# Quantised attention: where the probability-value products stand beside the transposes of turned tiles

## The chip, the cores and the metric

The kernel runs on one core of one Trainium2 chip. The metric is the device time of one execution in microseconds (us), lower is better. A core has a matmul engine (TensorE, PE in the profile, whose weight loads are shown as PEld), VectorE (DVE), ScalarE (ACT), GpSimd (POOL), and SyncE (SP), which here issues the DMAs. Each engine works through its own list of instructions in program order and waits on semaphores where it needs the work of another.

## The reference

Two layers over x (16 x 256 x 512) with a context (16 x 256 x 512). The first layer is where the change lies: two attentions of 16 heads with 32 channels each, both with fake-quantised q, k, probabilities and v.

```
def _attn(x, ctx, wq, wk, wv, wo, bo, dq, dk, dv, dw):
    q, k, v = heads(x @ wq), heads(ctx @ wk), heads(ctx @ wv)
    sim = einsum('bhid,bhjd->bhij', _fq(q, dq, 128, 8), _fq(k, dk, 128, 8)) * SCALE
    attn = softmax(sim)
    out = einsum('bhij,bhjd->bhid', _fq(attn, dw, 0, 8), _fq(v, dv, 128, 8))
    return merge_heads(out) @ wo + bo
h1 = _ln(x, ln1);  x = _attn(h1, h1, a1) + x
h2 = _ln(x, ln2);  x = _attn(h2, context, a2) + x
h3 = _ln(x, ln3);  x = gated feed-forward(h3) + x
```

The second layer is a plain cross attention of 8 heads with 64 channels each.

## The kernel before

**Stages.** The program has three stages, one behind the other, each over all 16 sequences: both quantised attentions (0 to about 1224 us), the first half of the feed-forward (to about 1826 us), and its second half together with the second layer (to the end). The change is in the first stage only.

**Phases and groups.** In the first stage a phase is the inner part of one attention of one sequence: eight groups (GROUPS) of two heads. For every group TensorE makes the scores (`pe_scores`, L503) in one of two PSUM tiles S; DVE takes the row maxima (L690), POOL makes the bias, ACT the exponentials with their sums (`act_exp`, L595), POOL and DVE the scaled and rounded probabilities pq (`dve_probs`, L698 to L715), SP turns them by a DMA transpose into pT (`turn_probs`, L916), and TensorE makes the products of probabilities and values (`pe_pv`, L525) in a PSUM tile O, three groups behind the scores.

**Fills.** The wide work of TensorE, projections (L157), output projections (L148) and transposes of 128 x 128 blocks (L132), is cut into "fills" of half a tile and laid into the groups by tables. Fill j = 0 goes to the PSUM bank PJ0 and j = 1 to PJ1 (for q2 the other way round). One round of the loop treats two phases, first `two_` (second attention of one sequence), then `one_` (first attention of a later sequence):

```
PHASE2_FILLS = {0: [("q1", 0)], 1: [("q1", 1)], 2: [("k1", 0)], 3: [("k1", 1)],
                4: [("ctxT", 0), ("ctxT", 1), ("o1", 0)], 5: [("o1", 1)], 6: [("v1", 0)], 7: [("v1", 1)]}
PHASE1_FILLS = {0: [("h2T", 0), ("h2T", 1), ("k2", 0)], 1: [("q2", 0)], 2: [("q2", 1)], 3: [("k2", 1)],
                4: [("o2", 0)], 5: [("o2", 1)], 6: [("v2", 0)], 7: [("hT", 0), ("hT", 1), ("v2", 1)]}
```

The fills ctxT, h2T and hT are the turned tiles: eight transposes of the context, of the normalised second input (from xhat of x1) and of the normalised next sequence (from xhat of x_in). `act_transposed` takes their first half out of PJ0 (L579 as a copy for ctxT; through `affine_act`, L179, for the others), and `dve_transposed` their second half out of PJ1 (L671, or `affine_dve`, L186). Both come in their engine's list ahead of the exponentials and the probabilities of the same group. xhat of x1 (`ln_xhat`, L124) comes in DVE's list at the end of group 7 of `two_`.

**Rounds.** Around the loop of 13 rounds stand the phases P_A and P_B ahead of it, a peeled round, and P_Y and P_Z behind it, with tables of their own. P_A has ctxT in group 4, P_B has h2T in group 5 and hT in group 7, P_Y has ctxT in group 0 and h2T in group 5.

**Order of TensorE in a group** (`pe_phase`): the scores of the next group; then the fills that are transposes; then the products of the group three back; then the other fills. A fill waits until its PSUM bank is emptied (`pj_emptied`), a transpose for its source as well, the products for the turned probabilities (`probs_turned`). A matmul that waits holds up all that stands behind it in this list.

Of the kernel before, what the change touches and what calls it, by code (L numbers as in the profile page):

```python
# [39 lines left out]
def build(nc, t, out):  # L40
# [3 lines left out]
    def sb(stack, name, shape, dt=F32):  # L44
        return stack.enter_context(nc.sbuf_tensor(name, shape, dt))
# [7 lines left out]
    with ctx:  # L53
# [73 lines left out]
        def transpose_chunks(bank, src, j):  # L127

            for c in range(2):
                for tt in range(TT):  # L130
                    k = 2 * j + c
                    last = nc.tensor.transpose(bank[:, c * TOK + tt * P:c * TOK + (tt + 1) * P],  # L132
                                               src[:, tt, k * P:(k + 1) * P], ident[:])
            return last
# [10 lines left out]
        def by_token(bank, w, xT, j):  # L145

            for k in range(KC):
                last = nc.tensor.matmul(bank[:], xT[:, k, j * P:(j + 1) * P], w[:, k, :],  # L148
                                        start=(k == 0), stop=(k == KC - 1))
            return last  # L150
# [79 lines left out]
        def bank_of(stage, name, j):  # L230

            return 1 - j if name == "q2" else j
# [4 lines left out]
        def before(stage, b, name, j):  # L237

            bank = bank_of(stage, name, j)
            n = fills_of(stage, bank).index((name, j))  # L240
            if stage != "first":
                n += len(fills_of("first", bank))
                n += len(fills_of("loop", bank)) * (b if stage == "loop" else ROUNDS)
            if stage == "last":
                n += len(fills_of("peeled", bank))
            return n
# [3 lines left out]
        def kind_of(name):  # L250
            return name.split("@")[0]
# [28 lines left out]
        def at(stage, b, name, j):  # L280
            return (stage, b, name, j)
# [13 lines left out]
        def turned_before(stage, b, name, j, kinds=TURNED):  # L295

            def those(s, fills=None):
                return [f[0] for f in (ORDER[s] if fills is None else fills)
                        if f[1] == 0 and kind_of(f[0]) in TURNED]
            n = 0  # L300
            if stage != "first":
                n += len(those("first")) + len(those("loop")) * (b if stage == "loop" else ROUNDS)
            if stage == "last":
                n += len(those("peeled"))
            here = those(stage, ORDER[stage][:ORDER[stage].index((name, j))])
            while here and kind_of(here[-1]) not in kinds:
                here.pop()
            return n + len(here)
# [26 lines left out]
        with ExitStack() as one:  # L335
# [12 lines left out]
            hT = sb(one, "hT", [P, 2, KC, TOK], F32R)  # L348
            ctxT = sb(one, "ctxT", [P, 2, KC, TOK], F32R)
# [90 lines left out]
            def ln_x1(b):  # L440
                return 2 * b + 2 if not (isinstance(b, int) and b == B - 1) else 2 * b + 1

            def ln_x(b):
                return 2 * b - 1


            def wait_weight(pe, name):

                pe.wait_ge(w_low_done, KC * (WEIGHTS.index(name) + 1))

            def pe_fill(pe, where):
                stage, b, name, j = where
                kind = kind_of(name)
                bank = bank_of(stage, name, j)
                n = before(*where)
                if not (isinstance(n, int) and n == 0):

                    pe.wait_ge(pj_emptied[bank], n)
                if kind == "hT" or kind == "h2T":
                    seq = {"hT@0": 0, "hT@1": 1, "hT": b + 3, "h2T": b + 1}[name]  # L460
                    m = 0 if name == "hT@0" else (1 if name == "hT@1" else (ln_x(seq) if kind == "hT" else ln_x1(seq)))
                    pe.wait_ge(ln["xhat_done"], TT * (m + 1))
                    ins = transpose_chunks(PJ[bank], xhat, j)
                elif kind == "ctxT":
                    seq = 0 if stage == "first" else b + 1
                    pe.wait_ge(ctx_loaded, 16 * (seq + 1))
                    ins = transpose_chunks(PJ[bank], ctx_in, j)
                elif kind in ("o1", "o2"):

                    if stage == "first":  # L470
                        done = 1
                    elif name == "o2@15":
                        done = 32
                    elif stage == "last":
                        done = 30 if kind == "o1" else 31
                    else:
                        done = 2 * b + (2 if kind == "o1" else 3)
                    pe.wait_ge(oT_done, 2 * done)
                    if stage == "first":
                        pe.wait_ge(wo_loaded[0], 16)  # L480
                    ins = by_token(PJ[bank], wo[0 if kind == "o1" else 1], oT, j)
                else:

                    from_ctx = kind in ("k2", "v2")
                    pe.wait_ge(turned_low_done, 2 * turned_before(*where, ("ctxT",) if from_ctx else ("hT", "h2T")))
                    w = "a" + kind[1] + "_w" + kind[0]
                    if stage == "first":
                        wait_weight(pe, w)
                    ins = (by_token_split if kind[0] == "v" else by_channel_split)(
                        PJ[bank], w1[w], ctxT if from_ctx else hT, j)  # L490
                ins.then_inc(pj_filled[bank], 1)

            def pe_scores(pe, ph, g):

                pe.wait_ge(quantised, ph.q_at[g // (GROUPS // 2)])
                if not (isinstance(ph.n, int) and ph.n == 0 and g < 2):

                    pe.wait_ge(exp_done, 4 * (ph.group(g) - 1))
                for i in range(2):
                    h = 2 * g + i  # L500
                    r = DH0 * (h % 4)
                    for qt in range(TT):
                        ins = nc.tensor.matmul(S[g % 2][:, i, qt, :],  # L503
                                               qT[ph.tiles][r:r + DH0, h // 4, qt * P:(qt + 1) * P],
                                               kT[ph.tiles][r:r + DH0, h // 4, :], start=True, stop=True)
                ins.then_inc(scores_done, 1)
# [6 lines left out]
            def pe_pv(pe, ph, g):  # L513
                pe.wait_ge(probs_turned[g % 2], turned_count(ph, g))
                if g == 0:
                    pe.wait_ge(quantised, ph.v_at)
                half = g // (GROUPS // 2)
                if g % (GROUPS // 2) == 0 and not (isinstance(ph.n, int) and ph.n == 0):

                    pe.wait_ge(oT_done, 2 * ph.n + half - 1)  # L520
                for i in range(2):
                    h = 2 * g + i
                    r = DH0 * (h % 4)
                    for kc in range(TT):
                        ins = nc.tensor.matmul(O[half][r:r + DH0, (h // 4) % 2, :],  # L525
                                               vQ[ph.tiles][:, kc, h * DH0:(h + 1) * DH0],
                                               pT[:, g % 2, 4 * i + kc:4 * i + kc + 3:2, :], start=(kc == 0),
                                               stop=(kc == TT - 1))
                ins.then_inc(pv_done, 1)

            def pe_phase(pe, ph, prev, nxt):
                for g in range(GROUPS):
                    if g + 1 < GROUPS:
                        pe_scores(pe, ph, g + 1)
                    elif nxt:
                        pe_scores(pe, nxt, 0)
                    fills = ph.steps(g)
                    for name, j in fills:
                        if kind_of(name) in ("hT", "h2T", "ctxT"):
                            pe_fill(pe, at(ph.stage, ph.b, name, j))  # L540
                    if g >= 3:
                        pe_pv(pe, ph, g - 3)
                    elif prev:
                        pe_pv(pe, prev, g + GROUPS - 3)
                    for name, j in fills:
                        if kind_of(name) not in ("hT", "h2T", "ctxT"):
                            pe_fill(pe, at(ph.stage, ph.b, name, j))

            def pe_drain(pe, ph):

# [1240 lines left out]
```

## Time and profile before

| | us |
|---|---|
| median of 3 runs | 3019.38 (3018.3 to 3019.39) |
| the profiled execution: its own time | 3019.96 |
| the profiled execution: span from first to last instruction | 3018.2 |
| PE busy over the span | 2806.9 (93%) |
| DVE busy | 1771.2 (59%) |
| ACT busy | 1455.2 (48%) |
| POOL busy | 692.1 (23%) |

The shares are means over three stages with different limits. In the first stage alone (0 to 1224 us) PE is busy for 1079.50 us and DVE for 1045.49 us. A busy PE is one with a matmul under way, not one at its peak.

### The profile page before, as it was taken

How to read it: one execution, taken by the hardware profiler on the slowest of the kernel's cores; microseconds unless marked ns; L12 is line 12 of the kernel's file. 1: busy time of each engine (PE TensorE's matmuls, PEld its weight loads, DVE VectorE, ACT ScalarE, POOL GpSimd, SP SyncE). 2: the span in 40 equal slices, each digit the busy share in tenths (PEclk: the TensorE clock that was granted, in tenths of full speed). 3: DMA queues.
4: the chain of work that ended last, by engine and by line, in shares of the span. 5: the costliest groups of instructions: out<-in, count | busy, mean ns of one | idle time of the engine just before them, and what ended most of it. 6: DMA issues, size and time to landing. Idle time of an engine off the chain costs nothing. (4 is left out here: it accounts for less than half of the span.)

```text
span 3018.2 us, 54146 instructions
## 1 busy us (share of the span) xinstructions
PE 2806.9 (93%) x17920; PEld 2214.6 (73%) x17920; DVE 1771.2 (59%) x4484; ACT 1455.2 (48%) x3763; POOL 692.1 (23%) x1147
## 2 busy tenths in 40 slices
PE   5799999999999996699999997999999999999997
PEld 5566666666666663599999996888888888888885
DVE  6799899999999986433333335344444444444432
ACT  4577777777777765211111112444444444444442
POOL 1222222222222221133333322112111111111110
PEclk8899999999999997799999998999999999999997
DMA  4443343333333342400010004000000000000000
GB/s 144 83 82 80 80 85 85 79 84 85 83 80 80 87 77 54 152 29 28 28 42 28 28 21 140 22 28 35 28 28 28 28 28 28 28 28 28 35 15 14
DMA packets 325753, 169.11 MB, mean 56 GB/s; under 512 B 274240, under 2 KB 290624, under 8 KB 325696
## 3 DMA queue, kind: packets, MB, share of 16 engines
q1 hardware_dynamic: 325696, 168.39, 22.0%
q8 instruction: 31, 0.51, 0.1%
q14 instruction: 26, 0.21, 0.0%
HBM read 76.07 MB, written 25.17 MB: 34 GB/s over the span
## 5 line engine op out<-in xcount | busy, mean ns | idle before, releaser
L595 ACT ACTIVATE e<-S,bias,qk_scale 128x256 f32<-128x256 f32 x1024 | 563.6, 564 | 65.3 <-DVE e L707 61.4
L690 DVE TENSOR_REDUCE negmax<-S 128x4 f32<-128x1024 f32 x256 | 312.0, 1219 | 105.3 <-PE S L503 103.7
L707 DVE TENSOR_SCALAR e<-e,rsum 128x256 f16<-128x256 f32 x1024 | 291.8, 348 | 2.5
L565 ACT ACTIVATE shifted<-PJ,round_col,inv 128x512 f32<-128x512 f32 x192 | 149.4, 778 | 227.5 <-PE PJ L157 226.5
L1584 POOL TENSOR_TENSOR mid_partsB<-mid_actB,mid_partsB 128x256 fp32r<-128x256 f32 x128 | 102.1, 797 | 611.8 <-DVE mid_partsB L1482 611.8
L148 PE MATMUL PJ<-w_a_wo,oT 128*128 128x512 f32 x512 | 239.6, 612 | 2.6 <-ACT oT L604 1.8
L157 PE MATMUL PJ<-hT,w_a_wq 128*128 128x256 f32 x1536 | 208.3, 294 | 21.5 <-DVE hT L685 17.7
L157 PEld LDWEIGHTS PJ<-hT,w_a_wq 128*128 128x128 f32 x1536 | 195.4, 199 | 35.5 <-issue 35.5
L595 ACT ACTIVATION_READ_ACCUMULATOR e<-S,bias,qk_scale 128x1 f32 x1024 | 209.1, 204 | 0.0
L157 PE MATMUL AG0A<-h_partsA,upA 128*128 128x256 f32 x1536 | 200.0, 287 | 7.2 <-POOL h_partsA L1579 3.4
L157 PE MATMUL AG0B<-h_partsB,upB 128*128 128x256 f32 x1536 | 199.1, 286 | 7.6 <-POOL h_partsB L1579 6.4
L157 PEld LDWEIGHTS AG0A<-h_partsA,upA 128*128 128x128 f32 x1536 | 192.1, 194 | 15.7 <-issue 10.0
L157 PEld LDWEIGHTS AG0B<-h_partsB,upB 128*128 128x128 f32 x1536 | 192.4, 192 | 11.6 <-issue 8.1
L157 PE MATMUL AG1A<-h_partsA,upA 128*128 128x256 f32 x1536 | 195.9, 284 | 4.4 <-DVE downA L1429 4.4
L157 PEld LDWEIGHTS AG1A<-h_partsA,upA 128*128 128x128 f32 x1536 | 193.2, 193 | 8.7 <-issue 4.8
L157 PEld LDWEIGHTS AG1B<-h_partsB,upB 128*128 128x128 f32 x1536 | 191.6, 191 | 9.2 <-issue 5.0
L157 PE MATMUL AG1B<-h_partsB,upB 128*128 128x256 f32 x1536 | 195.8, 284 | 0.0
L1584 POOL TENSOR_TENSOR mid_partsA<-mid_actA,mid_partsA 128x256 fp32r<-128x256 f32 x128 | 100.5, 785 | 383.8 <-DVE mid_partsA L1482 383.8
L793 POOL TENSOR_TENSOR bias<-negmax,qk_scale 128x4 f32<-128x4 f32 x256 | 76.3, 298 | 460.5 <-DVE negmax L690 457.1
L148 PEld LDWEIGHTS PJ<-w_a_wo,oT 128*128 128x128 f32 x512 | 93.8, 192 | 112.0 <-issue 108.0
L1374 ACT ACTIVATE gateA<-AG0A,cols_pack 128x256 f32<-128x256 f32 x64 | 30.4, 475 | 270.6 <-PE AG0A L157 270.6
L1475 DVE SCALAR_TENSOR_TENSOR mid_actB<-AG1B,cols_pack,gateB 128x256 f32<-128x256 f32 x64 | 31.0, 484 | 210.7 <-ACT gateB L1374 210.7
(186 smaller groups left out, 5578.8 us busy)
## 6 DMA issues: line engine op xcount, KB each, us to landing
x_in<-in_x_dram SPq DMA_DIRECT2D x16, 512.0 KB, 3.5
ctx_in<-in_ctx_dram SPq DMA_DIRECT2D x16, 512.0 KB, 3.5
mid_dram<-x SPq DMA_DIRECT2D x16, 512.0 KB, 2.7
y_inA<-mid_dram SPq DMA_DIRECT2D x16, 512.0 KB, 3.6
part_dram<-x3A SPq DMA_DIRECT2D x16, 512.0 KB, 4.0
y_inB<-mid_dram SPq DMA_DIRECT2D x16, 512.0 KB, 3.2
kv_in<-in_ctx_dram SPq DMA_DIRECT2D x16, 512.0 KB, 4.7
baseB<-part_dram SPq DMA_DIRECT2D x16, 512.0 KB, 3.2
```

Of the source, the lines that this page charges most:

```text
L148: last = nc.tensor.matmul(bank[:], xT[:, k, j * P:(j + 1) * P], w[:, k, :], start=(k == 0), stop=(k == KC - 1))
L157: last = nc.tensor.matmul(acc, lhs(l), rhs(r), start=(start and i == 0), stop=(stop and i == 2))
L565: nc.scalar.activation(shifted[:, bank, :], PJ[bank][:], ACT.Identity, bias=round_col[:, 0:1], scale=inv[:, d:d + 1]).then_inc(pj_emptied[ ...
L595: nc.scalar.activation(e[:, s, i, :], S[s][:, i // 2, i % 2, :], ACT.Exp, bias=bias[:, s, i:i + 1], scale=qk_scale[:, ph.a:ph.a + 1], accu ...
L690: nc.vector.tensor_reduce(negmax[:, g % 2, :], S[g % 2][:].rearrange("p i q n -> p (i q) n"), AX_X, ALU.max, negate=True).then_inc(max_don ...
L707: nc.vector.tensor_scalar(e16[:, s, i, :], e[:, s, i, :], rsum[:, s, i:i + 1], ROUND16, ALU.mult, ALU.add).then_inc(prob_scaled, 1)
L793: nc.gpsimd.tensor_tensor(bias[:, g % 2, :], negmax[:, g % 2, :], qk_scale4[:, ph.a, :], ALU.mult).then_inc(bias_done, 1)
L1374: nc.scalar.activation(gate[:, f % 2, :], AG[f % 2][:, TOK:2 * TOK], ACT.Gelu, bias=ff_b1[:, c:c + 1]).then_inc(gate_done, 1)
L1475: nc.vector.scalar_tensor_tensor(out=mid_act[:, f % 2, :], in0=AG[f % 2][:, 0:TOK], scalar=ff_b1[:, c:c + 1], in1=gate[:, f % 2, :], op0=A ...
L1584: nc.gpsimd.tensor_tensor(mid_parts[:, f % 2, 1, :], mid_act[:, f % 2, :], mid_parts[:, f % 2, 0, :], ALU.subtract).then_inc(mid_low_done, 1)
```

## The change

In every group of `pe_phase` the products of probabilities and values come directly behind the scores, and all fills of the group, transposes first as the tables list them, come behind the products. No instruction is added or taken away, and no other engine's list is changed. Groups without transposes keep their order.

```diff
                     elif nxt:
                         pe_scores(pe, nxt, 0)
-                    fills = ph.steps(g)
-                    for name, j in fills:
-                        if kind_of(name) in ("hT", "h2T", "ctxT"):
-                            pe_fill(pe, at(ph.stage, ph.b, name, j))
                     if g >= 3:
                         pe_pv(pe, ph, g - 3)
                     elif prev:
                         pe_pv(pe, prev, g + GROUPS - 3)
-                    for name, j in fills:
-                        if kind_of(name) not in ("hT", "h2T", "ctxT"):
-                            pe_fill(pe, at(ph.stage, ph.b, name, j))
+                    for name, j in ph.steps(g):
+                        pe_fill(pe, at(ph.stage, ph.b, name, j))
```

## Rows read from the trace of the kernel before

**Rows 1.** The page: TensorE's granted clock in 40 slices, tenths of full speed.
```profile
PEclk8899999999999997799999998999999999999997
```

**Rows 2.** Windows, two rounds: length; busy PE, PEld, DVE, ACT, POOL; clock, DMA, GB/s.
```profile
507.00:576.30 69.30, 65.16 (x426) 44.17 (x424) 64.01 (x165) 51.60 (x153) 17.78 (x41) 1.00 0.39 83
576.30:647.00 70.70, 66.62 (x427) 45.69 (x425) 64.04 (x165) 51.67 (x153) 18.23 (x41) 0.98 0.38 82
```

**Rows 3.** Waits, 141 to 1093 us: who waited for whom, us in total, times, longest.
```profile
PE PJ L132 <- DVE xhat L124: 27.8, 14, 2.0
PE PJ L157 <- DVE turned L186: 9.9, 13, 0.8
PE PJ L132 <- ACT shifted L565: 9.3, 13, 0.7
PE PJ L157 <- ACT turned L179: 6.6, 13, 0.5
PEld PJ L148 <- ACT turned L579: 3.0, 14, 0.2
ACT turned L579 <- PE PJ L132: 2.9, 14, 0.2
```

**Rows 4.** Timeline of PE, ctxT: start, us, what, count, [idle before <- releaser].
```profile
506.71 0.39 PE L503 MATMUL S<-kT,qT 32*128 32x256 bf16 x4
507.03 1.29 PE L132 MATMUL PJ<-ident,ctx_in 128*128 128x128 f32 x8
508.25 0.40 PE L525 MATMUL O<-pT,vQ 128*32 128x256 bf16 x4
508.57 3.70 PE L148 MATMUL PJ<-w_a_wo,oT 128*128 128x512 f32 x8
```

**Rows 5.** Timeline of ACT beside it.
```profile
506.83 0.78 ACT L565 ACTIVATE shifted<-PJ,round_col,inv 128x512 f32<-128x512 f32 x1 [0.18 <-PE PJ L157]
507.82 0.59 ACT L579 COPY turned<-PJ 128x512 f32<-128x512 f32 x1 [0.21 <-PE PJ L132]
```

**Rows 6.** Timeline of DVE between ctxT and h2T, the last wait and xhat.
```profile
516.94 1.22 DVE L690 TENSOR_REDUCE negmax<-S 128x4 f32<-128x1024 f32 x1 [0.64 <-PE S L503]
...
525.20 0.99 DVE L124 TENSOR_SCALAR xhat<-x,mv,rstd 128x512 f32<-128x512 f32 x2
```

**Rows 7.** Timeline of PE at h2T.
```profile
526.25 1.10 PE L132 MATMUL PJ<-ident,xhat 128*128 128x128 f32 x8 [1.98 <-DVE xhat L124]
...
528.18 3.12 PE L157 MATMUL PJ<-ctxT,w_a_wk 128*128 128x256 f32 x24 [0.51 <-ACT turned L179]
```

**Rows 8.** Timeline of ACT at h2T.
```profile
527.03 1.02 ACT L179 ACTIVATE turned<-PJ,cols_pack 128x256 f32<-128x256 f32 x2 [2.38 <-PE PJ L132]
```

**Rows 9.** Timeline of PE at hT.
```profile
555.88 1.09 PE L132 MATMUL PJ<-ident,xhat 128*128 128x128 f32 x8 [0.72 <-ACT shifted L565]
...
558.06 3.01 PE L157 MATMUL PJ<-w_a_wv,ctxT 128*128 128x512 f32 x12 [0.76 <-DVE turned L186]
```

**Rows 10.** SP's issue of turned probabilities; their landing, 590 to 736 us.
```profile
520.06 1.23 SPq L916 DMA_TRANSPOSE pT<-pq  x1
...
DMA to landing us min/median/max: 3.0/3.1/3.7
```

**Rows 11.** Windows with a fallen clock, columns as in rows 2.
```profile
176.00:178.00 2.00, 1.49 (x13) 1.05 (x13) 1.94 (x3) 1.25 (x3) 1.44 (x2) 0.89 0.70 131
...
1016.00:1018.00 2.00, 1.49 (x11) 1.04 (x10) 1.83 (x4) 1.86 (x4) 0.88 (x2) 0.81 0.57 105
```

**Rows 12.** Timeline of PE at h2T in two rounds with a fallen clock.
```profile
597.49 4.60 PE L157 MATMUL PJ<-ctxT,w_a_wk 128*128 128x256 f32 x24 [0.51 <-ACT turned L179]
...
1085.95 1.94 PE L132 MATMUL PJ<-ident,xhat 128*128 128x128 f32 x8 [2.02 <-DVE xhat L124]
...
1088.37 4.87 PE L157 MATMUL PJ<-ctxT,w_a_wk 128*128 128x256 f32 x24
```

**Rows 13.** Timeline of PE in P_Y, behind ctxT and its products.
```profile
1125.85 0.40 PE L503 MATMUL S<-kT,qT 32*128 32x256 bf16 x4 [2.85 <-ACT e L595]
```

## The prediction

> **What bounds the kernel now.** I read the page's clock line first. Its dips lie at the ends of stages, with short ones inside the first stage [rows 1]. Then I cut the first stage into rounds. A round of the loop lasts 69.30 us and TensorE is busy for 65.16 of them, DVE for 64.01; the next one lasts 70.70 with the same number of instructions to within one or two and a lower mean clock [rows 2]. So TensorE is the bound with DVE close behind, and what matters is TensorE's idle time. The table of waits over all rounds shows four kinds of it, each once a round: 27.8 us in front of the transposes of h2T (for DVE's xhat), 6.6 us behind them (for ACT to empty PJ0), 9.3 us in front of those of hT (for ACT), 9.9 us behind them (for DVE) [rows 3]. The timelines of single places then tell what each gate hangs on.
>
> **What the change moves.** In a round the four matmuls of one product group trade places with eight transposes at three points: h2T, hT, ctxT. A product group takes the issue of 0.32 us (508.25 to 508.57), as the scores do (506.71 to 507.03) [rows 4]. Nothing is added, so each point is a question of which gate ends last.
>
> h2T, 14 times (13 rounds and the peeled one). The products move into the idle time of 1.98 us in front of the transposes [rows 7]. They can run there: their turned probabilities were issued at 520.06 and land within 3.0 to 3.7 us [rows 10], so at 523.8 at the latest, while the products will stand at 526.25 - 1.98 = 524.3. Were they late, 1.65 us of the idle time would cover it. The transposes start with xhat, as before. Behind them k2 starts at 528.18, for it waits until ACT has emptied PJ0: ACT starts 0.78 us after the transposes' start and needs 1.02 us, to 528.05, and 0.13 later k2 starts [rows 7, 8]. That chain does not contain the products. Before, they lay inside it and cost nothing; now they lie in front of it and cost nothing. Idle time behind the transposes grows from 0.51 to 0.83 us, that in front shrinks from 1.98 to 1.65. Gain: 0. Bounds: a gain of 0.32 us if something in the chain behind should be quicker, no loss.
>
> hT, 14 times (P_B too). The same figure: 0.72 us idle in front, for ACT to empty PJ0, and 0.76 behind, for DVE to empty PJ1; v2 starts at 558.06, 2.18 us after the transposes' start [rows 9]. The products fit into the 0.72. Gain: 0, bounds again 0 to 0.32.
>
> ctxT. Here there is no idle time in front: scores, transposes, products and o1 stand behind one another at 506.71, 507.03, 508.25 and 508.57 [rows 4]. The gate of o1 is again PJ0, emptied by ACT's copy. ACT stood idle for 0.21 us until TensorE had filled it, started at 507.82, and took 0.59, to 508.41 [rows 5]; with the 0.13 to 0.16 us that such a gate takes, o1 was released at about 508.55, just when the products had been issued. The table says so for all rounds: o1's weight load waits 0.2 us for this copy 14 times, and the copy itself 0.2 us for the transposes 14 times [rows 3]. The products are now exactly the cover of that copy. Moved ahead of the transposes, they push the transposes from 507.03 to 507.36; the copy ends at 508.74, o1 starts at about 508.90. Cost: 0.33 us. Bounds: 0 (if the gate hides something the timeline does not show), 0.40 (the full duration of a product group, [rows 4]). I take 0.33, since both sides of the gate were tight.
>
> Is this slip given back later in the round? It would be if TensorE's wait for xhat, 1.98 us, took it up. DVE's last wait before xhat is the row at 516.94, for TensorE's scores of group 7; from there DVE works without a wait to xhat at 525.20 [rows 6]. Those scores stand behind o1, so they, xhat and the transposes of h2T all come 0.33 us later. From k2 on TensorE runs again into its own list. The slip stays, once in each of 14 rounds: 14 x 0.33 = 4.6 us.
>
> The edges. In P_A and at h2T in P_B TensorE waits long in front of the transposes, and the products move into that: 0. In P_Y, ctxT has no cover: the next scores wait for ACT's exponentials [rows 13], which stand behind the copy, so 0.2 to 0.3 us: I take 0.2. Queues: SP issues a transfer only when products two groups back are done; these now end earlier at h2T and hT and at ctxT too, so nothing of SP's or POOL's comes later for them. DVE's half of ctxT was at its start held by DVE's own maxima, and has a wait for scores behind it; it takes the delay up.
>
> **The clock.** The granted clock falls to the lower level, 1.2 GHz of 2.4, behind h2T: windows of seven rounds, every other one, from 176 to 1016 us have a mean between 0.89 and 0.81 [rows 11], and the peeled round at 1086 us has slow matmuls too [rows 12]. What TensorE did before is the same each time: two idle stretches, 1.98 and 0.51 us, with 1.4 us of transposes and products between. Rounds in between have the same stretches and keep 2.4 GHz, so this is a margin. A fall costs 70.70 - 69.30 = 1.40 us [rows 2]; k2 then takes 4.60 us [rows 12] where it takes 3.12 [rows 7]. In the peeled round the transposes took 1.94 us instead of 1.09 and k2 4.87 [rows 9, 12], together 2.6 us more. So 8 falls in 14 rounds cost 7 x 1.40 + 2.6 = 12.4 us. The regular "every other" hangs on the length of two rounds (140.0 us); a round 0.33 us longer breaks it. The sum of idle time at h2T stays 2.48 us but TensorE now works for 1.1 us rather than 1.4 between the two stretches, so they lie closer. I take two falls more: 2 x 1.40 = 2.8 us. Bounds: 0 falls (-12.4 us) and 14 (+8.4 us).
>
> The Trainium skill speaks against the change here. "TensorE: Matmul & The Clock Gate", section "A second HAM failure mode: psum-queue depth-cycling", says that micro-idles between groups of matmuls can be frequent enough for the clock to swing between its levels. The change adds a micro-idle of 0.33 us at ctxT and doesn't shorten the sum at h2T. By that rule every h2T would be followed by a fall, which is rival C; the trace so far agrees only in that falls stand behind two near idle stretches, and not behind each.
>
> **Sum.** 4.6 + 0.2 + 0 + 0 + 2.8 = 7.6 us, on the profiled execution's 3019.96 us: 3027.6. The median of the runs lies 0.6 us lower, so 3027.0 us.
>
> **Rivals.**
> A. The slip is absorbed. If DVE's chain before xhat had slack, or o1's release came from elsewhere, ctxT costs nothing and the clock's pattern stays: 3019.4 us, with part of it up to 3022. For it: 1.98 us of idle time stand right in front of h2T. Against it: DVE has no idle time between 516.94 and xhat [rows 6]. Chance 0.17.
> B. The slip comes, and the pattern of falls gets rarer, 5 instead of 8: 4.8 - 3 x 1.40 = +0.6, 3020.0 us. For it: TensorE's idle stretch in front of the transposes gets shorter. Against: the two lie closer. Chance 0.15.
> C. A fall behind every h2T: 4.8 + 6 x 1.40 = +13.2, 3032.6 us. Chance 0.10.
> D. Faster: the clock does not fall at h2T any more, because the products break the 1.98 us into a shorter stretch of 1.65. It decides once at least seven of the eight falls go: 4.8 - 12.4 = -7.6, 3011.8 us. A second road to the same side is a gate behind h2T and hT that opens earlier than shown, at most 28 x 0.32 = 9.0 us, less the 4.8. For: the falls are marginal. Against: the idle sum at h2T does not change. Chance 0.06.
>
> My own case keeps 0.52, with its own range 3024 to 3030. Seen as one scale, no change is what lies within 0.2% (6.0 us, about what a measurement of this kernel tells apart), so 3013.4 to 3025.4. Slower: most of the forecast (0.46) and C (0.10), 0.56. Same: A, B and the low edge of the forecast (0.06), 0.38. Faster: D, 0.06. The range 3019 to 3032 takes in A, B, the forecast and most of C.
>
> **What would show it.** In the changed kernel's timeline: at ctxT scores, products, transposes 0.33 us apart, then o1 with an idle time of about 0.3 us that ends with ACT L579, 14 times (some 4.6 us of a kind of wait that TensorE's table does not have now). At h2T idle time in front near 1.65 us, behind near 0.83; at hT 0.40 and 1.08; a round without a fall 69.63 us. Ten or so falls behind h2T. I am wrong in the step of ctxT if o1 follows the transposes without idle time or the clean round is still 69.30 us; wrong in h2T and hT if their idle sums (2.49 and 1.48 us) shrink; wrong on the clock if falls are fewer than 8.

## The result, and the profile after

The changed kernel is slower: a median of 3030.14 us (3027.72 to 3037.97, 6 runs) against 3019.39 us (3018.18 to 3021.98, 6 runs). The ratio is 1.0038, 95% interval 1.0025 to 1.0051. The profiled execution took 3031.61 us, 11.65 more than that of before. A fall is a stretch in which TensorE's granted clock drops from 2.4 to 1.2 GHz; a clean round is one without a fall, measured from one start of the h2T transposes to the next. A row below answers to the one named beside it; below L503 and the other lines of TensorE, line numbers are five smaller than before (L590 is the L595 of before).

The windows of two rounds behind one another, columns as in [rows 2]: the first has the full clock, the second a fall.

```profile
531.04:600.57 69.53, 65.06 (x425) 44.21 (x425) 64.07 (x166) 51.62 (x152) 18.01 (x41) 1.00 0.39 83
600.57:671.22 70.65, 66.24 (x424) 45.47 (x424) 64.08 (x166) 51.61 (x152) 18.03 (x41) 0.98 0.38 82
```

The clean round has grown from 69.30 to 69.53 us. That is 3.0 us in the 13 rounds between the first and the last h2T. The table of waits over 141 to 1100 us, against [rows 3]:

```profile
PE PJ L132 <- DVE xhat L124: 23.0, 14, 1.7
...
PE PJ L157 <- DVE turned L186: 14.2, 13, 1.1
...
PE PJ L157 <- ACT turned L179: 10.3, 14, 0.8
...
PEld PJ L148 <- ACT turned L574: 7.8, 14, 0.6
ACT turned L574 <- PE PJ L132: 7.5, 14, 0.5
...
PE PJ L132 <- ACT shifted L560: 5.0, 13, 0.4
PE PJ L148 <- ACT turned L574: 4.5, 14, 0.3
```

What is in front of the transposes has gone down by 4.8 us for xhat and 4.3 for ACT, and what is behind them has gone up by 3.7 and 4.3. The last line is new: 4.5 us, 14 times, TensorE idle in front of o1 (the first half of the output projection behind ctxT). In the timeline of TensorE at ctxT, and of ACT beside it (against [rows 4, 5]):

```profile
511.29 0.39 PE L503 MATMUL S<-kT,qT 32*128 32x256 bf16 x4
511.61 0.40 PE L525 MATMUL O<-pT,vQ 128*32 128x256 bf16 x4
511.94 1.09 PE L132 MATMUL PJ<-ident,ctx_in 128*128 128x128 f32 x8
513.36 1.55 PE L148 MATMUL PJ<-w_a_wo,oT 128*128 128x512 f32 x3 [0.33 <-ACT turned L574]
```

```profile
512.72 0.59 ACT L574 COPY turned<-PJ 128x512 f32<-128x512 f32 x1 [0.54 <-PE PJ L132]
```

From scores to o1 it is 2.07 us, where it was 1.86, so o1 stands 0.21 us later; the clean round shows 0.23. The copy ends at 513.31 and o1 starts 0.05 us later.

TensorE at h2T and at hT in a clean round (against [rows 7, 9]):

```profile
528.99 0.40 PE L525 MATMUL O<-pT,vQ 128*32 128x256 bf16 x4
531.04 1.09 PE L132 MATMUL PJ<-ident,xhat 128*128 128x128 f32 x8 [1.65 <-DVE xhat L124]
532.97 3.12 PE L157 MATMUL PJ<-ctxT,w_a_wk 128*128 128x256 f32 x24 [0.84 <-ACT turned L179]
...
560.67 1.09 PE L132 MATMUL PJ<-ident,xhat 128*128 128x128 f32 x8 [0.39 <-ACT shifted L560]
562.85 1.43 PE L157 MATMUL PJ<-w_a_wv,ctxT 128*128 128x512 f32 x5 [1.09 <-DVE turned L186]
```

From the transposes to k2 it is 1.93 us and to v2 2.18, to the hundredth what it was. The products moved out of one idle stretch into the other, and no start behind them moved.

The rest of the loss is the clock. The granted clock fell from 2.4 to 1.2 GHz behind h2T in 12 of 14 rounds (8 before), three times for a long stretch (1 before), and twice behind hT, where it never fell before. Three of the places, by the timeline of TensorE:

```profile
176.29 5.49 PE L157 MATMUL PJ<-ctxT,w_a_wk 128*128 128x256 f32 x24 [0.84 <-ACT turned L179]
...
246.80 1.81 PE L132 MATMUL PJ<-ident,xhat 128*128 128x128 f32 x8 [1.65 <-DVE xhat L124]
...
420.99 4.59 PE L157 MATMUL PJ<-w_a_wv,ctxT 128*128 128x512 f32 x12 [1.09 <-DVE turned L186]
```

k2 takes 3.12 us at the full clock, v2 3.01 and the transposes 1.09. Where the time went, from the starts of the h2T transposes, first to fourteenth: before 175.94 to 1085.95, 910.01 us; after 174.36 to 1097.12, 922.76 us. Of these 12.75 us, 13 x 0.23 = 3.0 are the longer clean round. The remaining 9.8 are falls: beyond clean rounds the 13 rounds held 9.1 us before and 18.9 after. Ahead of the first h2T 1.6 us were won, behind the last 0.5 lost; the cause of neither is known.

### The profile page after: what moved, and what is told of

Its sections match the earlier page's. It is cut to its first block and busy times, and to the rows that moved or that the text cites. A ratio compares the mean times of both kernels' runs of the same rounds, so it can differ in the third digit from the quotient of the medians.

```text
span 3029.8 us, 54146 instructions
## 1 busy us (share of the span) xinstructions
PE 2816.2 (93%) x17920; PEld 2223.9 (73%) x17920; DVE 1772.6 (59%) x4484; ACT 1455.4 (48%) x3763; POOL 690.5 (23%) x1147
## 5 line engine op out<-in xcount | busy, mean ns | idle before, releaser
L590 ACT ACTIVATE e<-S,bias,qk_scale 128x256 f32<-128x256 f32 x1024 | 563.7, 565 | 64.6 <-DVE e L702 60.2
L590 ACT ACTIVATION_READ_ACCUMULATOR e<-S,bias,qk_scale 128x1 f32 x1024 | 209.2, 204 | 0.0
```

Source lines behind the costliest of these rows:

```text
L590: nc.scalar.activation(e[:, s, i, :], S[s][:, i // 2, i % 2, :], ACT.Exp, bias=bias[:, s, i:i + 1], scale=qk_scale[:, ph.a:ph.a + 1], accu ...
```

## The experiments

Each run is compared with executions of the kernel before on the same chip. Their medians were 3020.43 us for the first four experiments of the table, 3021.25 for the next four (to the run with eight matmuls) and 3020.93 for the last four. The ratio is not simply that of the two medians. Clean rounds and falls are read from the one profiled execution of each; the clean round is a mean, good to about 0.01 us.

| run | median us | ratio, 95% interval | clean round us | falls at h2T, at hT |
|---|---|---|---|---|
| before | see above | 1 | 69.29 | 8, 0 |
| changed | 3030.14 | 1.0038 (1.0025, 1.0051) | 69.53 | 12, 2 |
| order at h2T and hT alone | 3021.08 | 1.0013 (0.9995, 1.0030) | 69.33 | 7, 0 |
| order at ctxT alone | 3028.56 | 1.0031 (1.0021, 1.0040) | none seen | 14, 0 |
| before, matmuls in the gap | 3014.46 | 0.9978 (0.9970, 0.9987) | 69.29 | 0, 4 |
| changed, matmuls in the gap | 3014.51 | 0.9980 (0.9972, 0.9989) | 69.49 | 0, 1 |
| products between halves | 3024.77 | 1.0009 (1.0000, 1.0018) | 69.20 | 12, 0 |
| k2 over the gap | 3073.76 | 1.0176 (1.0162, 1.0190) | see below | see below |
| two matmuls a round (0.26 us) | 3027.14 | 1.0023 (1.0013, 1.0033) | 69.57 | 10, 0 |
| eight matmuls a round (1.02 us) | 3040.63 | 1.0071 (1.0056, 1.0087) | none seen | 14, 0 |
| two shorter matmuls a round | 3036.20 | 1.0052 (1.0039, 1.0065) | 69.55 | 8, 0 |
| all gaps with matmuls | 3007.45 | 0.9955 (0.9942, 0.9968) | 69.22 | 0, 0 |
| xhat earlier | 3043.64 | 1.0070 (1.0058, 1.0082) | see below | see below |
| xhat earlier, between | 3042.25 | 1.0068 (1.0055, 1.0081) | see below | see below |

**The two halves of the change.** First the order at h2T and hT alone; the first of the two conditions in `pe_phase` is shown, and the second (`not in`) has the same tuple:

```diff
-                        if kind_of(name) in ("hT", "h2T", "ctxT"):
+                        if kind_of(name) in ("ctxT",):
```

> Products directly behind the scores at h2T and hT only; at ctxT the order of before. Theory 1 (the place of the products at h2T and hT brings falls of the clock, and nothing else): a round without a fall stays at 69.30 us, idle time at h2T is 1.65 in front and 0.84 behind, falls stand in 12 or so of 14 rounds instead of 8, time about 3019.4 + 8 = 3027 us. Theory 2 (the new idle time at ctxT, or the longer round that it makes, brings the falls): pattern of falls as before, 3019 us. Theory 3 (the reordering at h2T and hT costs stream time by itself): clean round longer than 69.30 us.

Then the order at ctxT alone, the same two lines with ("hT", "h2T") in place of ("ctxT",).

> Products directly behind the scores at ctxT only; at h2T and hT the order of before. Theory 1: clean round 69.52 us (0.22 us longer, o1 idle 0.33 us behind ctxT), falls about as before (7 to 10), time 3019.4 + 3 = 3022.5 us, up to 3025. Theory 2: falls in 12 or more rounds, 3028 us or above.

The first is no different from before that can be measured in ten of its twelve executions (3013.39 to 3023.07 us). The other two took 3041.90 and 3042.34 us, where no execution of the kernel before on that chip was above 3025.89; their granted clocks were the lowest of the twelve, 0.957 and 0.960 against 0.967 to 0.971. What sets those two apart is not known, for neither was profiled. The second has most of the loss by itself. Waits of TensorE over 141 to 1100 us with the order at h2T and hT alone:

```profile
PE PJ L132 <- DVE xhat L124: 23.2, 14, 1.7
PE PJ L157 <- DVE turned L186: 14.2, 13, 1.1
PE PJ L157 <- ACT turned L179: 11.6, 14, 0.8
PE PJ L132 <- ACT shifted L565: 5.0, 13, 0.4
```

It has the same idle stretches at h2T and hT as the changed kernel, and yet it falls in every other round, at 176, 316, 456 us and so on, as the kernel before does. So theory 1, that the place of the products in the gap brings falls, is refuted as the cause of the changed kernel's usual loss. At ctxT alone the gap at h2T is the old one (1.98 us in front, 0.51 behind), and the clock fell in each of the 14 rounds, four times for a long stretch:

```profile
318.69:389.52 70.83, 66.42 (x424) 45.68 (x424) 64.05 (x166) 51.61 (x152) 17.61 (x41) 0.97 0.38 81
672.88:744.53 71.65, 67.79 (x425) 46.70 (x425) 64.06 (x166) 51.61 (x152) 18.07 (x41) 0.95 0.38 81
```

**Is it the clock, or time of the order itself?** Ten matmuls whose results are overwritten hold TensorE busy in the gap at h2T, in the kernel before and in the changed one (the changed one's edit is shown):

```diff
+            def pe_keep_busy(pe, where, count=10):
+                stage, b, name, j = where
+                pe.wait_ge(pj_emptied[bank_of(stage, name, j)], before(*where))
+                for _ in range(count):
+                    nc.tensor.matmul(PJ[bank_of(stage, name, j)][:, 0:TOK], w1["a1_wq"][:, 0, 1, 0:P],
+                                     w1["a1_wq"][:, 0, 0, 0:TOK], start=True, stop=True)
...
+                    if ("h2T", 0) in ph.steps(g) and ph.stage in ("loop", "peeled"):
+                        pe_keep_busy(pe, at(ph.stage, ph.b, "h2T", 0))
```

> The kernel before, with ten matmuls (128x256, fp32r, of a weight tile by itself) written into the empty PJ0 in front of the transposes of h2T in the 13 rounds and the peeled one; their results are overwritten. Ten take 1.28 us at full clock and fit into the 1.98 us of idle time. Theory 1 (the idle time at h2T is what the clock falls after): no falls at h2T, all rounds 69.30 us, 3019.4 - 12 = 3007 us. Rival (falls have another cause, as the time since the last one): no change or, if a filler comes into the way, slower: 3019 to 3022 us.

> The changed kernel with the same ten matmuls, behind the products and in front of the transposes of h2T (1.28 us in the 1.65 us of idle time). Theory 1: no falls at h2T, clean rounds of 69.52 us, so 3 us above the run with the old order and the same fillers: 3010 us; falls behind hT (two in the changed kernel) may stay, up to 3014. Theory 3 (the order costs time beside the clock): 9 us or more above that run, 3017 us.

No fall at h2T is left in either, and the two orders, 11 us apart without the matmuls, have the same median (3014.46 and 3014.51). A clean round of each, old order first:

```profile
245.48:314.80 69.32, 66.56 (x435) 45.45 (x435) 64.02 (x166) 51.61 (x152) 17.81 (x41) 1.00 0.39 83
```

```profile
243.14:312.65 69.51, 66.43 (x434) 45.45 (x435) 64.03 (x166) 51.60 (x152) 17.60 (x41) 1.00 0.38 83
```

The 0.2 us a round are still there. In the profiled executions the old order had four falls behind hT, of about 1.5 us each, and the new one a single fall; but the old order's was the slowest of its twelve (3018.35 us), so its four falls may be more than its median has. Why the two medians agree to 0.1 us, where 14 x 0.2 = 2.8 should part them, stays open. The gain over before, 0.2%, is half of what I expected; the falls behind hT, of which the kernel before has none in its profiled execution, take part of it back.

**Idle time or length?** The order at ctxT makes two things: 0.33 us of idle time and a round that is some 0.23 us longer. So I made the round of the kernel before longer with work, in front of k1's first half, where its timeline shows no wait. Two matmuls (0.26 us), eight (1.02 us), and later two of 256 and 172 columns, meant as 0.215 us (the first one's edit is shown):

```diff
+            def pe_longer(pe, where, count=2):
+                stage, b, name, j = where
+                pe.wait_ge(pj_emptied[bank_of(stage, name, j)], before(*where))
+                for _ in range(count):
+                    nc.tensor.matmul(PJ[bank_of(stage, name, j)][:, 0:TOK], w1["a1_wq"][:, 0, 1, 0:P], ...)
...
+                        if (name, j) == ("k1", 0) and ph.stage in ("loop", "peeled"):
+                            pe_longer(pe, at(ph.stage, ph.b, name, j))
```

> The kernel before, with two matmuls (128x256, 0.26 us together) in front of k1's first half in each round, where TensorE is the bound; no idle time is added and nothing else changes. Theory length: clean round 69.55 us as with the changed order, the pattern of every other round breaks, 12 or more falls, 3019.4 + 3.6 + 6 = 3029 us. Theory idle (the 0.33 us of idle time at ctxT are what brings the falls): 8 falls as before, 3023 us.

> The same with eight matmuls, 1.02 us a round. Both theories: +14.3 us for the matmuls, clean round 70.3 us. Theory length: the number of falls changes again, between 4 and 14, by a rule that isn't 'longer is more'; if every round falls 3019.4 + 14.3 + 8.4 = 3042 us. Theory idle: 8 falls, 3034 us.

> The kernel before, with two matmuls of 256 and 172 columns (0.215 us) in front of k1's first half in each round: the length that the order at ctxT adds, but as work, without idle time. Theory length: clean round 69.51 us as with the order at ctxT alone, where the falls cost 19 us in 13 rounds; here too, 3020.5 + 3 + 6 = 3029 us. Theory that the idle time at ctxT has a share of its own in the falls: fewer of them, as in the run with 0.26 us of matmuls (11 us in 13 rounds), 3025 us.

All three cost more than the work put in. 0.26 us x 14 = 3.6 us of work cost 0.23% or 7 us (0.13 to 0.33%), and falls went to 10. 1.02 us x 14 = 14.3 us of work cost 21 us, with a fall in every round; one of the later ones:

```profile
888.05:959.71 71.66, 67.58 (x432) 46.64 (x432) 64.05 (x166) 51.54 (x152) 18.17 (x41) 0.98 0.38 81
```

The third missed its size: the clean round is 69.55 us, 0.26 longer than before, as good as that of the first. So the two are nearly one experiment made on two chips, and yet this one cost 0.52% or 16 us, more than the whole change. Its waits are those of before, no idle time added:

```profile
PE PJ L132 <- DVE xhat L124: 27.8, 14, 2.0
PE PJ L157 <- DVE turned L186: 9.9, 13, 0.8
PE PJ L132 <- ACT shifted L574: 9.3, 13, 0.7
PE PJ L157 <- ACT turned L179: 5.8, 12, 0.5
```

So new idle time isn't needed for the loss; a longer round is enough. But the length of the clean round alone does not fix the price, which was 7 us in one run and 16 in the other. Whether the chip has a share in that was not tested. The profiled execution of the third was the fastest of its six (3022.52 us against a median of 3036.20) and had 8 falls. That the rest of its time lies in the clock is seen in the mean granted clock of each execution: 0.968 in the profiled one, 0.960 to 0.963 in the five others (3034.88 to 3040.07 us). Where in the kernel those falls lie, no profile shows.

**Shorter instead of longer.** Products between the halves of ctxT:

```diff
+                    if ("ctxT", 0) in fills:
+                        pe_fill(pe, at(ph.stage, ph.b, "ctxT", 0))
...
-                        if kind_of(name) not in ("hT", "h2T", "ctxT"):
+                        if kind_of(name) not in ("hT", "h2T") and (name, j) != ("ctxT", 0):
```

> At ctxT the products stand between the two halves of the transposes: scores, ctxT 0, products, ctxT 1, o1; h2T and hT as before. The copy that opens PJ0 starts as early as before, and the second half no longer waits 0.21 us for PJ1. Gate reading: o1 opens with the copy's end, about 0.1 us earlier than before, clean round 69.18 us, and no new idle time of 0.33. Theory length (the falls follow from how the round's length sits against something periodic, whatever makes it longer or shorter): the pattern of every other round may break here too, 7 to 12 falls, 3018 to 3025 us. Theory idle (new idle time at ctxT brings falls): 7 or 8 falls, 3018 us.

The reading of the wait in front of o1 holds. TensorE at ctxT in a clean round:

```profile
505.76 0.39 PE L503 MATMUL S<-kT,qT 32*128 32x256 bf16 x4
506.08 0.66 PE L132 MATMUL PJ<-ident,ctx_in 128*128 128x128 f32 x4
506.67 0.40 PE L525 MATMUL O<-pT,vQ 128*32 128x256 bf16 x4
507.00 0.66 PE L132 MATMUL PJ<-ident,ctx_in 128*128 128x128 f32 x4
507.51 3.70 PE L148 MATMUL PJ<-w_a_wo,oT 128*128 128x512 f32 x8
```

o1 starts 1.43 us after the transposes' start instead of 1.54, and a clean round is 0.09 us shorter. But the pattern breaks on this side too: 12 falls, and the kernel ends no faster than the one of before (0.09% above it, interval 0.00 to 0.18%).

**Two versions that were to win more, and lost.** Useful work over the gap, by the tables. The bank of q2 and the count of `phase2` are adapted to it, and DVE has one more semaphore wait, in front of k2's second half, whose share was not measured by itself:

```diff
-  6: [("v1", 0)], 7: [("v1", 1)]}
+  6: [("v1", 0)], 7: [("v1", 1), ("k2", 0)]}
-  0: [("h2T", 0), ("h2T", 1), ("k2", 0)], 1: [("q2", 0)], 2: [("q2", 1)], 3: [("k2", 1)],
+  0: [("h2T", 0), ("h2T", 1), ("k2", 1)], 1: [("q2", 0)], 2: [("q2", 1)],
```

> Of the loop's and the peeled round's tables alone: k2's first half moves to group 7 of the second attention, where it covers the wait for xhat, its second half stands behind the transposes of h2T, and group 3 of the first attention is empty of fills. Useful work of 3.1 us lies over the idle 1.98 us. Theory gap (that wait bounds the round): the idle time at h2T goes, the next wait is q2's, for DVE's hT, some 0 to 1 us; round 67 to 68 us, few falls, 14 x 1.8 + 8 = 33 us less, 2986 us. Rival (DVE, busy 64.0 of 69.3 us, takes over at once because its list is not changed): round 69 us, only the falls go, 3010 us; slower than before if the group without a fill makes scores wait.

Neither theory's number: rounds of 73.0 to 74.5 us. The wait for xhat is gone, and the last half-sentence of the expectation came true. In TensorE's waits the scores in the group without a fill stand first, 3.1 us in each round, as much as the useful work moved:

```profile
PE S L503 <- ACT e L595: 39.8, 13, 3.1
PE PJ L157 <- DVE turned L186: 19.8, 26, 0.8
```

Then xhat ahead of the probabilities in DVE's list:

```diff
+                    if ("o1", 1) in ph.steps(5) and g == 7:
+                        ln_xhat(dve, ln, x1, xhat, ln_x1(ph.b + 1))
                     fills = [f for f in late(ph, prev, g) if kind_of(f[2]) in QUANTISED]
...
-                        if g == 7:
-                            ln_xhat(dve, ln, x1, xhat, ln_x1(ph.b + 1))
```

> The kernel before, with DVE's xhat of x1 ahead of the probabilities of group 6 in its list, at 523.3 instead of 525.2 us of the round looked at (POOL's rstd ends at 523.2). TensorE's order as before. The transposes of h2T start up to 1.9 us earlier. If TensorE's waits for DVE at h2T bound the round as told: clean round 67.5 us, falls few, 14 x 1.8 + 8 = 33 us less, 2987 us. If ACT, whose exponentials wait for the probabilities that now come 1 us later, takes over: round 69 us or more, 3010 to 3025 us.

> The same with the products between the halves of ctxT: 0.11 us a round less than with xhat earlier alone, 1.5 us in all, 2985 us, if the falls are as few in both.

The transposes of h2T start without a wait, and the round still grew to 71.8 us with a fall in it; the one round without a fall (822.02 to 892.30) is 70.28 us, 1.0 longer than the clean round before. The work behind them waits now for the probabilities that xhat pushed back, as the waits of the first of the two show (14 rounds, 141 to 1100 us):

```profile
PE O L525 <- DMA pT<-pq: 25.2, 27, 1.0
...
PE S L503 <- ACT e L595: 8.5, 13, 0.7
```

The clock falls there instead: mostly 12 to 13 us behind the start of h2T, in three rounds some 35, and never right at it. With the products between the halves of ctxT as well, the rounds are 71.7 us, the expected 0.1 shorter, and the falls stand in the same place. So the 1.98 us in front of h2T can't be had by moving xhat alone: DVE then delays the probabilities, and TensorE waits for those.

**The version that beats both.** Products between the halves of ctxT, twelve of the overwritten matmuls in front of h2T and four, into PJ1, in front of hT.

> Products between the halves of ctxT, twelve matmuls into the empty PJ0 in front of h2T, four into the empty PJ1 in front of hT (0.51 us in 0.72 us of idle time). Clean round 69.18 us, no falls at h2T and none at hT: 3020.5 - 12 - 1.5 = 3007 us. If falls at hT hang on the idle time behind its transposes, some of them stay: 3012 us.

It came out as expected: 3007.45 us, 0.45% (0.32 to 0.58) below before. Here are TensorE in its gap, and the windows of one round and of all rounds, the second with a clock of 1.00 for 933 us:

```profile
517.98 1.70 PE L535 MATMUL PJ<-w_a_wq 128*128 128x256 f32 x12
520.04 1.09 PE L132 MATMUL PJ<-ident,xhat 128*128 128x128 f32 x8 [0.36 <-DVE xhat L124]
```

```profile
243.12:312.38 69.26, 67.25 (x441) 46.20 (x441) 64.09 (x166) 51.55 (x152) 16.94 (x41) 1.00 0.39 83
141.00:1074.00 933.00, 906.49 (x5932) 622.89 (x5932) 862.60 (x2226) 693.54 (x2046) 233.21 (x555) 1.00 0.40 84
```

## Why the prediction was right, and where its sizes were off

**h2T and hT cost nothing: right.** Idle 1.65 and 0.84, 0.39 and 1.09 us, where 1.65 and 0.83, 0.40 and 1.08 were forecast. By itself this half has a ratio of 1.0013 (0.9995, 1.0030), with two executions of twelve 22 us above the others that the forecast has no place for.

**ctxT costs what the products covered: right in mechanism, mis-sized.** The new wait for ACT's copy is there 14 times with 0.33 us. But o1 moved by 0.21 us and the clean round by 0.23, not 0.33: some 3 us for 4.6. I gave the gate (the wait that releases o1) 0.13 to 0.16 us from the copy's end to the matmul's start and so took the old order as exactly tight. The changed kernel shows 0.05 us. So before, by this estimate, the gate opened at 508.46, and o1 stood for 0.11 us behind the issue of the products. Idle time seen after a change is not the delay by it: the part that was covered before must be taken off.

**The slip isn't absorbed at h2T: right.** The clean round is 69.53 us against 69.30, though 1.98 us of idle time stand in it (rival A falls). The run with xhat earlier shows from the other side that this idle time hangs on DVE's chain.

**The clock: right in kind, far too small.** The term that was mis-sized is "two falls more", 2.8 us. The rounds held 9.8 us more of it: four more falls at h2T, two at hT, and two more of the long kind, which cost more than 1.40 us (k2 at 5.49 us, or slow transposes ahead of it). The price of a short fall was about right: 9.1 us for seven of them is 1.3 each. It is the count and the kind that were off, and falls at hT had no term at all. The reason that I gave, that a longer round breaks the pattern of every other round, is what the runs with added work and the one with a shorter round bear out; the reason I gave beside it, that the two idle stretches lie closer, is refuted by the run with the order at h2T and hT alone. As to the rule of the Trainium skill ("TensorE: Matmul & The Clock Gate", section "A second HAM failure mode: psum-queue depth-cycling"): that small idle stretches between groups make the clock swing is what filling them shows (no fall at h2T in three runs). That the added one at ctxT does it isn't shown, since 0.26 us of work in place of the 0.33 us of idle time cost as much or more. Rival C, a fall behind every h2T at 3032.6 us, was as near as my own case: 12 falls at h2T lie halfway between 10 and 14, and 3030.14 us lies 2.5 below it and 3.1 above mine. It is what the order at ctxT alone did.

**Sum.** 3.0 for ctxT in the 13 rounds, 9.8 for the clock in them, -1.1 for what lies ahead and behind: 11.7 us, where I had 7.6. The direction came from ctxT, as forecast; the size mostly from what its 0.23 us did to the clock. That the total is off by only 4 us is in part luck: the clock cost 7.0 us more than I had, and the slip with the edges 2.9 less. The median lies just outside my own range of 3024 to 3030, and inside the wide one.

**What stays open.** Why a given length of the round brings 8, 10, 12 or 14 falls; I have a handful of lengths, not a rule. The same length brought 7 and 16 us, and single executions of one kernel differ by 18 us (3022.52 to 3040.07 with the two shorter matmuls) and by 29 (3013.39 to 3042.34 with the order at h2T and hT alone). Whether the idle time at ctxT has a small share of its own. And whether the falls at hT, which came in the changed kernel and in both runs with matmuls at h2T alone, have another cause than the rest. They were absent with four matmuls in front of hT, but that run also had the products between the halves of ctxT, so the two are not told apart.

## What to carry to other kernels

Before moving an instruction, look at which wait ends last behind it, not at the idle time it leaves or enters: work that stands between a producer and the wait of its consumer is cover, and moving it out costs what it covered. In a loop like this one, in whose rounds the clock sometimes falls behind an idle stretch of TensorE and sometimes not, price a change of the round's length not by its own time alone but by the falls before and after, and run it many times: 3.0 to 3.6 us of longer rounds cost 7 to 16 here. If such a stretch can't be closed, try overwritten matmuls in it.

## What the runs showed of the hardware

- A quarter of a microsecond of pure work a round (0.26 us of 69.3, 3.6 us in all) cost 7 us in one run and 16 in another, with no new wait in TensorE's table of waits in the second.
- The falls of the clock can lock to the rounds: in the kernel before every second one, 140 us apart, seven times in a row; with 1.02 us more work every one, the last nine rounds 71.61 to 71.67 us long.
- Single executions of one kernel on one chip can lie some 20 us apart, and the granted clock goes with it: with the order at h2T and hT alone ten of twelve ended by 3023.07 us with a mean granted clock of 0.967 to 0.971, two at 3042 with 0.957 and 0.960.
- Ten matmuls of no use, about 1.3 us of work a round, made the kernel before 0.22% (0.13 to 0.30%) faster; sixteen and a better order at ctxT 0.45%.
- A long fall costs about twice a short one: with the order at ctxT alone, rounds of 71.6 to 71.7 us against 70.4 to 70.9 (the first round apart), where a clean round of the changed kernel, with the same order there, is 69.5.
